# Half slots split their up weights on chip, and the rows of the next slot are turned inside the up products

## The chip, the cores and the metric

One NeuronCore of a Trainium2 chip runs the whole program. The metric is the device time of one execution in microseconds (us); a kernel's time is the median of its runs. The profiler records single executions, and every row below is of one such execution of the kernel before. The engines are PE (TensorE), DVE (VectorE), ACT (ScalarE), POOL (GpSimd) and SP (SyncE, which issues loads).

## The reference

4096 rows of 256 numbers go through four layers, each added to its own input: cross-attention, a mixture of experts with capacity, cross-attention, and a mixture in which each row goes to its two best of eight experts. Only the last one is touched:

```python
def _L1_ffn_ref(x, Wg, W11, W12, W2):          # Wg 256x8, W11/W12 8x256x512, W2 8x512x256
    gate_scores = softmax(x @ Wg)
    topk_scores, topk_idx = top_k(gate_scores, 2)
    topk_scores = topk_scores / (topk_scores.sum(-1, keepdims=True) + 1e-08)
    gate  = einsum('bsh,ehi->bsei', x, W11)
    value = einsum('bsh,ehi->bsei', x, W12)
    fused = gate * sigmoid(gate) * value
    expert_out = einsum('bsei,eih->bseh', fused, W2)
    gathered = take_along_axis(expert_out, topk_idx[..., None], axis=2)
    return sum(topk_scores[..., None] * gathered, axis=2)
x = x + _L1_ffn_ref(_layernorm(x), ...)
```

## The kernel before

The stage is `experts_top2` (lines 1342 to 1843); it begins at about 757 us of the trace and runs to the end. The 8192 pairs of a row and an expert have been sorted by expert in device memory. They are worked off in 32 **full slots** of 256 rows and 7 **half slots** of 128 rows, each slot of one expert. A loop of 7 passes (`body`) treats four full slots a, a+1, a+2, a+3 (a = 4j) and half slot j; `last` treats the remaining four. Products are in fp32 made of two parts: each factor is split into a "hi" copy and a "lo" rest, and three products (hi by hi, lo by hi, hi by lo) stand for one.

A full slot is, on PE: 4 transposes that turn its rows (L1481), `up` in four steps m = 0 to 3 of 12 matmuls (L1508), `down` of 24 matmuls (L1543). A half slot has 2 transposes (L1489), `half_up` of 12 matmuls 128x512 (L1521), a turn back (L1530) and `half_down` (L1555). PE's order in a pass is written out by hand:

```python
up(a);    transposes(a+1); down(a-1)
up(a+1);  transposes(a+2); down(a)
up(a+2);  half_transposes(j); down(a+1); half_up(j); transposes(a+3); down(a+2); half_turn(j)
up(a+3);  transposes(a+4); half_down(j)
```

Around it, for each full slot: ACT does the SiLU of each step m (L1632) and the hi copies of w2 (L1610), of the turned rows (L1614; half slot L1618) and of the hidden values (L1624). DVE multiplies gate and value (`hf`, L1752), does six small steps on weights and destinations (L1716 to L1721), and takes the lo rests: w2 (L1694), hidden values (L1689), rows (L1699; half slot L1704); it scales the outputs (L1738). POOL adds the scaled outputs to the result by indirect DMAs (`add`, L1812; half slot L1819). SP loads the sorted rows (L1435; half slot L1443), up weights of 2 MB per expert, already split into hi and lo in device memory (L1420, only when the expert changes), and w2 of 512 KB (L1428, likewise); before each it reads entries of a small table into registers (`entry`, L1404).

The up weights of a half slot, 2 MB, also come already split, in 8 pieces of 256 KB that ACT issues (L1599, queue q10): two at the fourth slot of the pass before, then two in each of a, a+1 and a+2. Its w2 comes in two pieces (L1605). Those of half slot 0 are issued ahead of the first slot. `half_up` waits for all 8 pieces.

The turned rows (xT_hi, xT_lo) have one buffer, so the rows of the next slot are turned only after `up` is over, and their split on ACT and DVE stands behind `up` too.

Of the kernel before, what the change touches and what calls it, by code (L numbers as in the profile page):

```python
# [15 lines left out]
P = 128  # L16
# [6 lines left out]
E = 8  # L23
# [14 lines left out]
NT1 = NF + NH + 1  # L38
# [429 lines left out]
def attention(p, layer, ins, setup, base, before):  # L468
# [423 lines left out]
    def plan(q):  # L892
# [51 lines left out]
        q.tensor_scalar(p.tab[:, 0, NF:NT1], row_o, float(IDLE_ROW), None, ALU.min).then_inc(s_tab, 1)  # L944
# [397 lines left out]
def experts_top2(p, ins, rows_from):  # L1342
# [11 lines left out]
    xT_hi, xT_lo = (at(k, x, [P, KC, T1], F32R) for k, x in ((56 + HALF, "xT_hi"), (58 + HALF, "xT_lo")))  # L1354
# [19 lines left out]
    hxin = at(60.5, "half_xin", [P, DW])  # L1374
    hxT_hi, hxT_lo = (at(k, x, [P, KC, P], F32R) for k, x in ((62 + HALF, "half_xT_hi"), (63 + HALF, "half_xT_lo")))
    hsg, hhf = (at(k, x, [P, F1]) for k, x in ((65, "half_sg"), (67, "half_hf")))
# [8 lines left out]
    sh_mt, sh_add = S("half_meta_steps"), S("half_rows_added")  # L1385
# [28 lines left out]
    def sync(q):  # L1414
        def load_up(i, par):
            e = entry(q, 1, i, E - 1)
            new = entry(q, 2, i, 1)
# [5 lines left out]
        def load_w2(i, par):  # L1423
            e = entry(q, 1, i, E - 1)
            new = entry(q, 2, i, 1)
# [4 lines left out]
        def load_x(i, par):  # L1430
            r = entry(q, 0, i, IDLE_ROW)
# [12 lines left out]

        def loads(i, par):
            load_x(i, par)
            load_up(i, par)
            load_w2(i, par)

        def body(j):  # L1450
            if not is_int(j):
                loads(4 * j + 1, 1)
            loads(4 * j + 2, 0)
            half_load_x(j)
            loads(4 * j + 3, 1)
            loads(4 * j + 4, 0)

        def last(a):
            for k in range(1, 4):
                loads(a + k, k % 2)  # L1460
        q.wait_ge(s_ahead, 16 * 4)
        q.wait_ge(rows_from.s_tab, 2)
        for i in range(2):
            load_up(i, i)
            load_w2(i, i)
        q.wait_ge(rows_from.s_tab, 3)
        rows_from.rows_landed(q)
        rows_from.tails_landed(q)
        for i in range(2):
            load_x(i, i)  # L1470
        slots(q, body, last)

    def tensor(q):
# [18 lines left out]
        def up(i, par, half=None, between=None):  # L1492
# [4 lines left out]
            for m in range(FC):  # L1497
                if m == 3 and between:
                    between()
                if m == 2 and half is not None:  # L1500
                    q.wait_ge(sh_hlo, half + 1)
                wait(q, s_hf, i * FC + m - 3)
                for v in range(2):
                    bank = ps[:, UP_BANK + m, v * T1:(v + 1) * T1]
                    k = 0
                    for c in range(KC):
                        for w, x in ((0, xT_hi), (0, xT_lo), (1, xT_hi)):
                            mm = q.matmul(bank, up_w[:, par, v, w, c, m * P:(m + 1) * P], x[:, c, :],  # L1508
                                          start=(k == 0), stop=(k == 3 * KC - 1))
                            k += 1  # L1510
                mm.then_inc(s_up, 1)

        def half_up(j):
            q.wait_ge(sh_xTlo, j + 1)
            q.wait_ge(sh_w, 16 * 8 * (j + 1))
            for v in range(2):
                q.wait_ge(s_hf, (4 * j + 2) * FC + v + 1)
                k = 0
                for c in range(KC):
                    for w, x in ((0, hxT_hi), (0, hxT_lo), (1, hxT_hi)):  # L1520
                        mm = q.matmul(ps[:, UP_BANK + v, :], x[:, c, :], hup[:, v, w, c, :],  # L1521
                                      start=(k == 0), stop=(k == 3 * KC - 1))
                        k += 1
                mm.then_inc(sh_up, 1)
# [34 lines left out]
        def body(j):  # L1559
            a = 4 * j  # L1560
            up(a, 0)
            transposes(a + 1, 1)
            if not is_int(j):
                down(a - 1, 1, j - 1)
            up(a + 1, 1)
            transposes(a + 2, 0)
            down(a, 0)
            up(a + 2, 0)
            half_transposes(j)
            down(a + 1, 1)  # L1570
            half_up(j)
            transposes(a + 3, 1, j)
            down(a + 2, 0)
            half_turn(j)
            up(a + 3, 1, j)
            transposes(a + 4, 0)
            half_down(j)

        def last(a):
            for k in range(3):  # L1580
                up(a + k, k % 2)
                transposes(a + k + 1, 1 - k % 2)
# [10 lines left out]
    def scalar(q):  # L1593
        def half_load_up(j, e, piece):

            v, w, c = piece // 4, piece // 2 % 2, piece % 2
            wait(q, sh_up, 2 * j)
            land(q, j)
            q.dma_start(hup[:, v, w, c, :].bitcast(F32), p.up1[e, :, v, w, c * F1:(c + 1) * F1]).then_inc(sh_w, 16)  # L1599

        def half_load_w2(j, e, piece):
            m = slice(piece * FC // 2, (piece + 1) * FC // 2)
            wait(q, sh_w2lo, j)
            land(q, j)
            q.dma_start(hw2[:, m, :], w2_d[:, e, m, :]).then_inc(sh_w2, 16)  # L1605
# [6 lines left out]
        def split_x(i, par):  # L1612
            q.wait_ge(s_xT, i + 1)
            q.activation(xT_hi[:, :, :], ps[:, X_BANK:X_BANK + KC, 0:T1], ACT.Copy).then_inc(s_xThi, 1)  # L1614
# [11 lines left out]
        def full(i, par, behind, ahead=None):  # L1626
            for m in range(FC):
                if ahead:
                    ahead(m)
# [11 lines left out]
        def half(j):  # L1641
# [10 lines left out]
        def body(j):  # L1652
            a = 4 * j
            e = None if is_int(j) else entry(q, 1, NF + j, E - 1)

            def ahead(first):
                def pieces(m):
                    if m % 2 == 1:
                        half_load_up(j, e, first + m // 2)
                    if m == 2 and first < 6:  # L1660
                        half_load_w2(j, e, first // 2 - 1)
                return None if is_int(j) else pieces

            def ahead_next(m):
                if m % 2 == 1:
                    half_load_up(j + 1, e_next, m // 2)
            full(a, 0, lambda: split_x(a + 1, 1), ahead(2))
            full(a + 1, 1, lambda: split_x(a + 2, 0), ahead(4))
            full(a + 2, 0, lambda: half_split_x(j), ahead(6))
            half(j)  # L1670
            e_next = entry(q, 1, NF + j + 1, E - 1)
            full(a + 3, 1, lambda: split_x(a + 4, 0), ahead_next)
# [5 lines left out]
        e = entry(q, 1, NF, E - 1)  # L1678
        for piece in range(8):
            half_load_up(0, e, piece)  # L1680
        for piece in range(2):
            half_load_w2(0, e, piece)
        slots(q, body, last)
        q.wait_ge(sh_w, 16 * (8 * NH + 2))

    def vector(q):
# [58 lines left out]
        def full(i, par, behind, output, between=False):  # L1745
            small = meta(i, par)
            for m in range(FC):
                if m == 3 and between:
                    output()
                q.wait_ge(s_sg, i * FC + m + 1)  # L1750
# [8 lines left out]
            behind()  # L1759
# [9 lines left out]
        def half(j):  # L1769
# [4 lines left out]
            split_x(4 * j + 3, 1)  # L1774
# [12 lines left out]
        def body(j):  # L1787
# [3 lines left out]
            full(a + 2, 0, lambda: half_split_x(j), lambda: outputs(a + 1, 1))  # L1791
# [11 lines left out]
    def gpsimd(q):  # L1803
# [17 lines left out]

        def body(j):
# [3 lines left out]
            add(a, 0)  # L1826
            add(a + 1, 1)
# [112 lines left out]
```

## Time and profile before

| | us |
|---|---|
| median of 3 runs | 1140.29 |
| the runs | 1137.93, 1140.29, 1145.8 |
| profiled execution, its own time | 1142.97 |
| its span | 1141.2 |
| the stage `experts_top2`, from the load of its first rows | 766.84 to the end |
| a pass with no weight load in its way (start of up(20) to start of up(24)) | 40.13 |

The mean granted clock of TensorE over the span is 0.964 of full speed. In the stage PE is busy for 92% of the time, DVE 64%, ACT 44%, POOL 30%.

### The profile page before, as it was taken

To read this page: it belongs to the slowest core of one execution; us is meant where nothing else is said; L and a number is where in the kernel's file an instruction comes from. 1 tells how busy PE (TensorE), PEld (TensorE's weight loads), DVE (VectorE), ACT (ScalarE), POOL (GpSimd) and SP (SyncE) were. 2 spreads that over 40 slices of the span, in tenths; PEclk is the share of its full clock that TensorE was granted. 3 is DMA by queue.
4 is the path that set the end of the run, shared out by engine and by line. 5 is a ranking of instruction groups with operands and counts; after the bars stand their busy time and mean duration, and the time that the engine had idled before them with its cause. 6 is when DMAs were issued, how large, how long until landed. Compare 5 with 4: busy or idle time off the path is not lost.

```text
span 1141.2 us, 24748 instructions
## 1 busy us (share of the span) xinstructions
PE 1033.3 (91%) x7562; PEld 955.1 (84%) x7562; DVE 720.7 (63%) x2241; ACT 661.5 (58%) x2450; POOL 509.4 (45%) x520
## 2 busy tenths in 40 slices
PE   6999998899999999889999999618999999899895
PEld 4688887799999998569999998617999989799795
DVE  6778886444444444866777777544756657576573
ACT  2788886444444443589999999304434444344351
POOL 1346776433333333345688886631232332333233
PEclk9999999899999999999999999757999999999898
DMA  9910002666666656101122221644868686757973
GB/s 315 341 52 25 29 30 72 259 223 226 220 228 221 226 187 202 34 20 38 48 72 74 71 69 55 255 149 122 243 143 285 161 268 179 209 141 232 320 222 71
DMA packets 101312, 180.69 MB, mean 158 GB/s; under 512 B 12898, under 2 KB 72932, under 8 KB 98788
## 3 DMA queue, kind: packets, MB, share of 16 engines
q1 hardware_dynamic: 71972, 133.13, 33.8%
q0 software_dynamic: 16368, 26.23, 10.5%
q10 hardware_dynamic: 12880, 20.21, 5.3%
q8 instruction: 44, 0.72, 0.3%
q14 instruction: 48, 0.39, 0.1%
HBM read 164.30 MB, written 62.43 MB: 199 GB/s over the span
## 4 chain that ended last, share of the span: by engine, by line
PE 75%; DMA 7%; DVE 7%; issue 4%; ACT 3%; SPq 2%; POOL 1%; ACTq 0%; DVEq 0%; POOLq 0%
PE psum L1508 12%; PE psum L696 11%; PE psum L679 11%; PE psum L1184 10%; PE psum L1201 10%; PE psum L1543 5%; DMA E_up_w<-up 4%; PE psum L651 4%; PE psum L1521 2%; DMA E_half_up_w<-up 2%; ACT L_prob L746 2%; PE psum L702 2%; PE psum L388 1%; DVE L_m_lo L440 1%; PE psum L666 1%
## 5 line engine op out<-in xcount | busy, mean ns | idle before, releaser
L746 ACT ACTIVATE L_prob<-psum,L_neg_max 128x64 f32<-128x64 f32 x768 | 229.3, 364 | 4.8 <-DVE L_neg_max L1003 4.7
L1812 POOL DMA_INDIRECT out<-E_y,E_dest x64 | 100.4, 1569 | 236.5 <-DVE E_y L1738 126.2
L1508 PE MATMUL psum<-E_xT_hi,E_up_w 128*128 128x256 f32 x1024 | 191.6, 286 | 14.3 <-DMA E_up_w<-up 7.3
L746 ACT ACTIVATION_READ_ACCUMULATOR L_prob<-psum,L_neg_max 128x1 f32 x768 | 196.3, 258 | 0.0
L1508 PEld LDWEIGHTS psum<-E_xT_hi,E_up_w 128*128 128x128 f32 x1024 | 162.3, 193 | 17.8 <-issue 11.6
L1508 PE MATMUL psum<-E_xT_lo,E_up_w 128*128 128x256 f32 x512 | 144.8, 283 | 0.0
L696 PE MATMUL psum<-L_n_hi,L_pT_hi 128*128 128x256 f32 x384 | 109.5, 285 | 9.8 <-DVE L_pT_lo L1010 9.8
L1632 ACT ACTIVATE E_sg<-psum 128x256 f32<-128x256 f32 x128 | 49.1, 384 | 117.7 <-PE psum L1508 109.8
L778 POOL TENSOR_TENSOR L_prob<-L_prob,L_rcp 128x512 f32<-128x512 f32 (+1 forms) x64 | 94.4, 1476 | 42.6 <-DVE L_rcp L969 41.2
L696 PE MATMUL psum<-L_n_hi,L_pT_lo 128*128 128x256 f32 x384 | 108.5, 282 | 0.0
L696 PE MATMUL psum<-L_n_lo,L_pT_hi 128*128 128x256 f32 x384 | 108.4, 282 | 0.0
L1242 ACT ACTIVATE E_h_hi<-psum 128x256 fp32r<-128x256 f32 (+1 forms) x128 | 55.7, 438 | 85.7 <-PE psum L1184 85.7
L1508 PEld LDWEIGHTS psum<-E_xT_lo,E_up_w 128*128 128x128 f32 x512 | 98.6, 193 | 0.0
L1752 DVE TENSOR_TENSOR E_hf<-psum,E_sg 128x256 f32<-128x256 f32 x128 | 53.9, 421 | 70.7 <-ACT E_sg L1632 68.9
L1285 DVE SCALAR_TENSOR_TENSOR E_h_lo<-psum,E_h_hi 128x256 fp32r<-128x256 f32 (+1 forms) x128 | 62.6, 491 | 53.8 <-ACT E_h_hi L1242 53.1
L1201 PE MATMUL psum<-E_w_hi,E_h_hi 128*128 128x256 f32 x320 | 90.0, 281 | 0.0
L1201 PE MATMUL psum<-E_w_hi,E_h_lo 128*128 128x256 f32 x320 | 89.4, 279 | 0.0
L1201 PE MATMUL psum<-E_w_lo,E_h_hi 128*128 128x256 f32 x320 | 89.4, 279 | 0.0
L696 PEld LDWEIGHTS psum<-L_n_hi,L_pT_hi 128*128 128x128 f32 x384 | 74.1, 193 | 13.5 <-issue 10.8
L679 PE MATMUL psum<-L_m_hi,L_xT_hi 128*128 128x512 f32 x192 | 81.9, 427 | 2.0 <-ACT L_prob L746 2.0
L1184 PE MATMUL psum<-E_xT_hi,E_w_hi 128*128 128x384 f32 (+1 forms) x256 | 78.8, 308 | 1.4 <-DVE E_xT_lo L1277 1.4
L1184 PE MATMUL psum<-E_xT_hi,E_w_lo 128*128 128x384 f32 (+1 forms) x256 | 78.8, 308 | 0.0
(248 smaller groups left out, 3141.1 us busy)
## 6 DMA issues: line engine op xcount, KB each, us to landing
E_up_w<-up SPq DMA_DIRECT2D x34, 2048.0 KB
E_w<-in_w SPq DMA_DIRECT2D x34, 512.0 KB
E_w<-in_w SPq DMA_DIRECT2D x16, 1024.0 KB, 7.2
E_half_up_w<-up ACTq DMA_DIRECT2D x58, 256.0 KB
E_xin<-rows SPq DMA_DIRECT2D x32, 260.0 KB
E_raw<-in_w SPq DMA_DIRECT2D x16, 512.0 KB, 6.6
up<-E_raw_hi SPq DMA_DIRECT2D x16, 512.0 KB, 6.3
up<-E_raw_lo SPq DMA_DIRECT2D x16, 512.0 KB, 4.0
```

The lines of the kernel that those rows point to most:

```text
L679: mm = e.matmul(bank, a[:, (t + 3) % 2, c, :], m[:, b, c, q * 512:(q + 1) * 512], start=(layer == 1 and c == 0 and j == 0), stop=(c == KC ...
L696: mm = e.matmul(o, a[:, r, :], m[:, b, r, :], start=(r == 0 and j == 0), stop=(r == PR - 1 and j == 2))
L746: last = e.activation(prob[q][:, h * KEYS:(h + 1) * KEYS], scores_ps(t)[:, h * KEYS:(h + 1) * KEYS], ACT.Exp, bias=nmx[:, q, h, :], accum_ ...
L778: e.tensor_tensor(pr, pr, rc[:, q, :, :].to_broadcast([P, H, KEYS]), ALU.mult).then_inc(s_p, 1)
L1184: mm = q.matmul(bank, a[par][:, c, m * P:(m + 1) * P], x[:, c, c0 * P:(c0 + cn) * P], start=(k == 0), stop=(k == 3 * KC - 1))
L1201: mm = q.matmul(bank, a[:, h, m, c * P:(c + 1) * P], w[par][:, m, :], start=(k == 0), stop=(k == 3 * FC - 1))
L1242: q.activation(h_hi[:, h, m, 0:cn * P], ps[:, UP_BANK + m % 4, 0:cn * P], ACT.Relu).then_inc(s_hhi, 1)
L1285: q.scalar_tensor_tensor(h_lo[:, h, m, 0:cn * P], ps[:, UP_BANK + m % 4, 0:cn * P], 0.0, h_hi[:, h, m, 0:cn * P].bitcast(F32), ALU.max, AL ...
L1508: mm = q.matmul(bank, up_w[:, par, v, w, c, m * P:(m + 1) * P], x[:, c, :], start=(k == 0), stop=(k == 3 * KC - 1))
L1543: mm = q.matmul(ps[:, Y_BANK + c, 0:D], a[:, par, m, c * P:(c + 1) * P], w[:, par, m, :], start=(k == 0), stop=(k == 3 * FC - 1))
L1752: q.tensor_tensor(hf[:, m, :], ps[:, UP_BANK + m, T1:2 * T1], sg[:, m, :], ALU.mult).then_inc(s_hf, 1)
L1812: q.indirect_dma_start(p.out[:, :], bass.IndirectOffsetOnAxis(ap=dest[:, par, c, :], axis=0), y[:, par, c, :], None, compute_op=ALU.add).t ...
```

## The change

It touches `experts_top2`, and the width of the table that `plan` writes (39 entries of slots in place of 40).

1. **Half slots' up weights.** Four raw pieces of 256 KB of w11 and w12 (1 MB) are loaded in place of eight split ones, issued by ACT after m = 1 and m = 3 of slots a and a+1. They are split on chip in slot a+2: ACT makes a hi copy of one piece after each step m (`half_split_up`), the first waiting for all four pieces; POOL takes the four lo rests, in its order behind the `add` of slot a and ahead of that of a+1. `half_up` waits for the four lo rests. w2 of the half slot is one load of 512 KB, issued at m = 1 of slot a+2. Nothing is loaded ahead of the first slot any more.
2. **Turned rows.** xT has two buffers. The transposes of slot i+1 stand at m = 2 inside up(i) (`turn`), their hi copy behind ACT's second SiLU, their lo rest ahead of DVE's third `hf`. In slot a+2 it is the half slot's transposes that stand there; those of a+3 come straight after up(a+2), ahead of down(a+1) and half_up, and they wait for the half slot's lo rest (`sh_xTlo`), since they write the same PSUM banks.
3. **SP.** The loads of up weights and w2 share one pair of table entries; entries are read ahead of the waits; those of the first two rows are read before the wait for the rows.

```diff
 def half_load_up(j, e, piece):
-    v, w, c = piece // 4, piece // 2 % 2, piece % 2
-    wait(q, sh_up, 2 * j)
+    v, c = piece // KC, piece % KC
+    wait(q, sh_wlo, 4 * j)
     land(q, j)
-    q.dma_start(hup[:, v, w, c, :].bitcast(F32), p.up1[e, :, v, w, c * F1:(c + 1) * F1]).then_inc(sh_w, 16)
+    q.dma_start(hraw[:, v, c, :], ins[("w11", "w12")[v]][e, c * P:(c + 1) * P, :]).then_inc(sh_w, 16)
+def half_split_up(j, piece):                      # ACT
+    v, c = piece // KC, piece % KC
+    q.wait_ge(sh_w, 16 * 4 * (j + 1))
+    wait(q, sh_up, 2 * j)
+    q.activation(hup[:, v, 0, c, :], hraw[:, v, c, :], ACT.Copy).then_inc(sh_whi, 1)
+def half_split_up(j, piece):                      # POOL
+    v, c = piece // KC, piece % KC
+    q.wait_ge(sh_whi, 4 * j + piece + 1)
+    q.tensor_tensor(hup[:, v, 1, c, :], hraw[:, v, c, :], hup[:, v, 0, c, :].bitcast(F32),
+                    ALU.subtract).then_inc(sh_wlo, 1)
 # PE
 def half_up(j):
     q.wait_ge(sh_xTlo, j + 1)
-    q.wait_ge(sh_w, 16 * 8 * (j + 1))
+    q.wait_ge(sh_wlo, 4 * (j + 1))
 def body(j):
-    up(a, 0)
-    transposes(a + 1, 1)
+    up(a, 0, turn=lambda: transposes(a + 1, 1))
     if not is_int(j):
         down(a - 1, 1, j - 1)
-    up(a + 1, 1)
-    transposes(a + 2, 0)
+    up(a + 1, 1, turn=lambda: transposes(a + 2, 0))
     down(a, 0)
-    up(a + 2, 0)
-    half_transposes(j)
+    up(a + 2, 0, turn=lambda: half_transposes(j))
+    transposes(a + 3, 1, j)
     down(a + 1, 1)
     half_up(j)
-    transposes(a + 3, 1, j)
     down(a + 2, 0)
     half_turn(j)
-    up(a + 3, 1, j)
-    transposes(a + 4, 0)
+    up(a + 3, 1, j, turn=lambda: transposes(a + 4, 0))
     half_down(j)
 # ACT, full(): in the loop over m
                 if m == 0:
                     split_w2(i, par)
+                if m == 1:
+                    behind()
                 if 0 < m < 3:
                     hidden_hi(i, par, m - 1)
-            behind()
+                if weights:
+                    weights(m)
 # DVE, full(): in the loop over m
+                if m == 2:
+                    behind()
                 q.wait_ge(s_sg, i * FC + m + 1)
 ...
-            behind()
 # POOL, body()
     add(a, 0)
+    for piece in range(4):
+        half_split_up(j, piece)
     add(a + 1, 1)
 # SP
-        load_x(i, par)
-        load_up(i, par)
-        load_w2(i, par)
+        r, e, new = entry(q, 0, i, IDLE_ROW), entry(q, 1, i, E - 1), entry(q, 2, i, 1)
+        load_x(i, par, r)
+        load_weights(i, par, e, new)
```

## Rows read from the trace of the kernel before

**Rows 1.** Page: the span, and the chain that ended last, by engine.
```profile
span 1141.2 us, 24748 instructions
PE 75%; DMA 7%; DVE 7%; issue 4%; ACT 3%; SPq 2%; POOL 1%; ACTq 0%; DVEq 0%; POOLq 0%
```

**Rows 2.** Windows: us; PE, PEld, DVE, ACT, POOL busy; clock; DMA share; GB/s.
```profile
768.00:1124.00 356.00, 327.70 (x2614) 318.24 (x2615) 229.45 (x686) 156.34 (x346) 105.09 (x67) 0.96 0.72 208
999.19:1039.32 40.13, 39.88 (x334) 39.10 (x335) 29.28 (x90) 19.77 (x44) 13.97 (x9) 1.00 0.56 124
```

**Rows 3.** Lines of PE, 768 to 1124 us: busy, mean ns, idle before and its releasers.
```profile
L1508 PE MATMUL psum<-E_xT_hi,E_up_w 128*128 128x256 f32 x1021 | 191.1, 286 | 14.3 <-DMA E_up_w<-up 7.3 <-DVE E_xT_lo L1699 6.8
...
L1521 PE MATMUL psum<-E_half_up_w,E_half_xT_hi 128*128 128x512 f32 x56 | 22.1, 458 | 12.5 <-DMA E_half_up_w<-up 12.5
```

**Rows 4.** Chain that ended last: start, us, step.
```profile
783.62 8.18 PE psum L1508 x48
...
871.67 10.44 DMA E_up_w<-up
...
975.90 7.18 DMA E_half_up_w<-up
983.21 4.60 PE psum L1521 x12
999.19 5.92 PE psum L1508 x48
...
1005.54 2.74 PE psum L1543 x24
1008.28 5.44 PE psum L1508 x48
...
1025.39 2.80 PE psum L1521 x12
...
1072.94 5.48 PE psum L1521 x12
```

**Rows 5.** Timeline of SP before the first slot (start, us, line; q: an issue).
```profile
760.94 0.12 SPq L1420 DMA_DIRECT2D E_up_w<-up  x1
762.51 0.09 SPq L1428 DMA_DIRECT2D E_w<-in_w  x1
...
766.84 0.41 SPq L1435 DMA_DIRECT2D E_xin<-rows  x1
```

**Rows 6.** Timeline of ACT and PE at slots 0 and 1; in brackets the idle before.
```profile
771.35 3.85 ACTq L1599 DMA_DIRECT2D E_half_up_w<-up  x8
...
776.61 1.28 ACT L1632 ACT_TABLE_LOAD   x1 [5.33 <-issue]
...
783.62 0.58 PE L1508 MATMUL psum<-E_xT_hi,E_up_w 128*128 128x256 f32 x1 [3.87 <-DVE E_xT_lo L1699]
```

**Rows 7.** Timeline of PE: first matmuls behind a wait, later in the stage.
```profile
907.10 0.38 PE L1508 MATMUL psum<-E_xT_hi,E_up_w 128*128 128x256 f32 x1 [0.24 <-DVE E_xT_lo L1699]
937.07 0.50 PE L1521 MATMUL psum<-E_half_up_w,E_half_xT_hi 128*128 128x512 f32 x1 [1.45 <-DMA E_half_up_w<-up]
983.21 0.79 PE L1521 MATMUL psum<-E_half_up_w,E_half_xT_hi 128*128 128x512 f32 x1 [4.92 <-DMA E_half_up_w<-up]
1072.94 0.79 PE L1521 MATMUL psum<-E_half_up_w,E_half_xT_hi 128*128 128x512 f32 x1 [4.64 <-DMA E_half_up_w<-up]
```

**Rows 8.** Timeline of ACT, DVE and POOL in slot 22 (its up runs from 1016.85).
```profile
1018.58 1.05 ACT L1610 ACTIVATE E_w_hi<-E_w 128x1024 fp32r<-128x1024 f32 x1
1020.61 0.16 DVE L1719 SCALAR_TENSOR_TENSOR E_mb<-E_xin,shift 128x2 f32<-128x2 f32 x1
1020.68 1.22 DVE L1694 TENSOR_TENSOR E_w_lo<-E_w,E_w_hi 128x1024 fp32r<-128x1024 f32 x1
1021.82 0.42 DVE L1689 TENSOR_TENSOR E_h_lo<-E_hf,E_h_hi 128x256 fp32r<-128x256 f32 x1
1023.42 0.41 DVE L1704 TENSOR_TENSOR E_half_xT_lo<-psum,E_half_xT_hi 128x256 fp32r<-128x256 f32 x1
1019.24 1.55 POOL L1812 DMA_INDIRECT out<-E_y,E_dest  x1 [0.30 <-issue]
```

**Rows 9.** Timeline of ACT in slot 14 (its up runs from 926.66).
```profile
931.01 1.06 ACT L1610 ACTIVATE E_w_hi<-E_w 128x1024 fp32r<-128x1024 f32 x1 [2.25 <-DMA E_w<-in_w]
```

**Rows 10.** One source line of POOL: count, then ns min/median/max and span.
```profile
L1322 POOL TENSOR_TENSOR E_raw_lo<-E_raw,E_raw_hi x16: 2396/2404/2419, 223.9 to 435.5; 128x1024 fp32r<-128x1024 f32 x16
```

**Rows 11.** Timeline of DVE and POOL, and the source line of this DVE instruction.
```profile
494.51 1.27 DVE L1018 SCALAR_TENSOR_TENSOR x<-L_got,factor,x 128x256 f32<-128x256 f32 x1
493.60 1.91 POOL L778 TENSOR_TENSOR L_prob<-L_prob,L_rcp 128x1024 f32<-128x1024 f32 x1 [8.68 <-DVE L_rcp L969]
L1018 DVE SCALAR_TENSOR_TENSOR x<-L_got,factor,x x32: 451/454/1273, 459.2 to 683.7; 128x256 f32<-128x256 f32 x32
```

More of the change, by code:

```diff
@@ L1353, in experts_top2 @@
     w2_hi, w2_lo = (at(k, x, [P, 2, FC, D], F32R) for k, x in ((40, "w2_hi"), (48, "w2_lo")))
[L1354 removed]
+    xT_hi, xT_lo = (at(k, x, [P, 2, KC, T1], F32R) for k, x in ((56 + HALF, "xT_hi"), (60 + HALF, "xT_lo")))
     xin = at(82, "xin", [P, 2, TC, DW])
@@ L1384, in experts_top2 @@
         S("half_" + x) for x in ("up", "silu", "h", "hT", "hT_hi", "hT_lo", "down", "y_scaled"))
-    sh_mt, sh_add = S("half_meta_steps"), S("half_rows_added")
+    sh_mt, sh_add, sh_whi, sh_wlo = (S("half_" + x) for x in ("meta_steps", "rows_added", "w1_hi", "w1_lo"))
     def nth(i):
@@ L1414, in sync, with load_weights @@
     def sync(q):
-        def load_up(i, par):
-            e = entry(q, 1, i, E - 1)
-            new = entry(q, 2, i, 1)
+        def load_weights(i, par, e, new):
             wait(q, s_up, FC * (i - 1))
@@ L1428, in load_w2, with load_x @@
             q.dma_start(w2[:, par, :, :], w2_d[:, e, :, :], cond=new).then_inc(s_w2[par], 16)
-        def load_x(i, par):
-            r = entry(q, 0, i, IDLE_ROW)
+        def load_x(i, par, r):
             wait(q, s_mt, NM * (i - 1))
@@ L1463, in sync @@
         for i in range(2):
-            load_up(i, i)
-            load_w2(i, i)
+            load_weights(i, i, entry(q, 1, i, E - 1), entry(q, 2, i, 1))
         q.wait_ge(rows_from.s_tab, 3)
+        r = [entry(q, 0, i, IDLE_ROW) for i in range(2)]
         rows_from.rows_landed(q)
@@ L1490, in half_transposes, with up @@
             mm.then_inc(sh_xT, 1)
-        def up(i, par, half=None, between=None):
+        def up(i, par, half=None, turn=None, between=None):
             q.wait_ge(s_xTlo, i + 1)
@@ L1497, in up @@
             for m in range(FC):
+                if m == 2 and turn:
+                    turn()
                 if m == 3 and between:
@@ L1580, in last @@
             for k in range(3):
-                up(a + k, k % 2)
-                transposes(a + k + 1, 1 - k % 2)
+                up(a + k, k % 2, turn=lambda: transposes(a + k + 1, 1 - k % 2))
                 down(a + k - 1, 1 - k % 2, NH - 1 if k == 0 else None)
@@ L1613, in split_x @@
             q.wait_ge(s_xT, i + 1)
-            q.activation(xT_hi[:, :, :], ps[:, X_BANK:X_BANK + KC, 0:T1], ACT.Copy).then_inc(s_xThi, 1)
+            q.activation(xT_hi[:, par, :, :], ps[:, X_BANK:X_BANK + KC, 0:T1], ACT.Copy).then_inc(s_xThi, 1)
         def half_split_x(j):
@@ L1624, in hidden_hi, with full @@
             q.activation(h_hi[:, par, m, :], hf[:, m, :], ACT.Copy).then_inc(s_hhi, 1)
-        def full(i, par, behind, ahead=None):
+        def full(i, par, behind, weights=None):
             for m in range(FC):
-                if ahead:
-                    ahead(m)
                 q.wait_ge(s_up, i * FC + m + 1)
@@ L1653, in body, with load, split @@
             a = 4 * j
[L1654 to L1669, printed above, removed]
+            e = entry(q, 1, NF + j, E - 1)
+            def load(first):
+                return lambda m: half_load_up(j, e, first + m // 2) if m % 2 else None
+            def split(m):
+                half_split_up(j, m)
+                if m == 1:
+                    half_load_w2(j, e)
+            full(a, 0, lambda: split_x(a + 1, 1), load(0))
+            full(a + 1, 1, lambda: split_x(a + 2, 0), load(2))
+            full(a + 2, 0, lambda: half_split_x(j), split)
+            split_x(a + 3, 1)
             half(j)
-            e_next = entry(q, 1, NF + j + 1, E - 1)
-            full(a + 3, 1, lambda: split_x(a + 4, 0), ahead_next)
+            full(a + 3, 1, lambda: split_x(a + 4, 0))
         def last(a):
@@ L1677, in scalar @@
         split_x(0, 0)
[L1678 to L1682, printed above, removed]
         slots(q, body, last)
-        q.wait_ge(sh_w, 16 * (8 * NH + 2))
     def vector(q):
```

35 lines of the change are left out of this document (15 added, 20 removed).

## The prediction

> **What bounds the kernel now.** I read the chain that ended last first: three quarters of the span is PE [rows 1], so a gain must come out of PE's idle time or out of work taken off PE. The change takes none off: the matmuls and transposes are as many as before. So I looked next at the windows: in the stage PE is busy for 327.7 of 356.0 us, at a clock of 0.96, and in a pass that no weight load disturbs for 39.9 of 40.1 us [rows 2]. The reader is to see that everything the change can give lies in those 28 us and in the clock. The lines of PE say where they are: 12.5 us ahead of half_up, all of it for pieces of the half slot's weights; 7.3 us ahead of up for its own weights; 6.8 us ahead of up for the lo rest of the turned rows [rows 3]. The chain shows what a wait costs beyond itself: half_up takes 2.80 us after none, 4.60 after the wait of 4.92, 5.48 after that of 4.64; up takes 5.44 in the flow and 5.92 behind a short wait [rows 4, 7].
>
> **What the change takes away.**
>
> - SP's start. SP issues five loads between 760.94 and 766.84, each up weight or w2 load 1.5 us after the one before, the last after 1.3 [rows 5]; two table entries stand in each step of 1.5, one in the last. Two pairs go, one entry moves ahead: at about 0.55 each that is 4 less 1, 1.6 us (bounds 0, if another wait stands there too, and 2.2).
> - The start of ACT. Ten issues hold ACT from 771.35 to 776.6, then a table load of 1.28; slot 0's chain of SiLU, hf and split comes that much later, PE waits 3.87 us for up(1), which then takes 8.18 instead of 5.92 [rows 4, 6]. Both go: 3.9 + 2.3 = 6.2.
> - The waits for turned rows at the end of a pass: 0.24 [rows 7], six like it of 0.24 to 0.29, 1.5 in all; the up behind each drops from 5.92 to 5.44 [rows 4], 6 x 0.48 = 2.9.
> - half_up's waits for pieces: 12.5 [rows 3], and the two slow half_ups, 1.8 + 2.7 = 4.5 [rows 4]. The lo rests that it waits for now are made in slot a+2; their cover is checked below. 17.0.
> - Up's waits for its own weights, 7.3 [rows 3]: half slots load 1 MB instead of 2 per pass, but these waits stand where 2 MB loads take 10.44 us to land [rows 4], and that stays so. I take 4 (bounds 0 and 7.3).
>
> Together 33.2 us.
>
> **What it adds.** In a pass PE now goes from up(a+2) straight to the transposes of a+3, and these wait for the half slot's lo rest. PE works in order, so down(a+1) and half_up stand behind this wait, and nothing covers it. Before, down(a+1), 2.74 us, lay between. What that rest waits for is a chain over ACT, DVE and POOL:
>
> Slot 22 shows it without loads in the way. Counted from the start of its up (1016.85): w2's hi copy ends at 2.8; DVE takes w2's lo rest from 3.8 to 5.05, a lo rest of hidden values to 5.4, then hf; the half rows' rest at present is done at 7.0; POOL's add ends at 3.9 [rows 8]. Up ends at 5.44. In the new order the half rows are turned at m = 2 and their rest stands behind w2's lo and the first h lo. ACT's first copy of 128x512 goes in between, about 0.6 (half of the 1.05 of 128x1024 [rows 8], with some fixed part), so hf and w2's lo come 0.6 later, at 4.4; the rest would be ready at 4.4 + 1.22 + 0.42 + 0.41 less overlaps, about 6.0: PE idles 0.6 us.
>
> But POOL now works in the same stretch. A subtract of 128x1024 takes it 2.40 us [rows 10], so each of the four of 128x512 about 1.2, and they start right behind the add, at 4.0. The trace has one place where DVE begins an instruction with two inputs in SBUF while such a POOL instruction runs: POOL runs from 493.60 to 495.51, DVE's instruction, else 0.45, takes 1.27 and ends 0.27 after POOL's [rows 11]. It was kept waiting for the whole of POOL's. w2's lo rest and the h lo rests have two inputs in SBUF. So I count, as the likeliest order: first subtract 4.0 to 5.2; DVE's last small step, which has SBUF inputs too, is held until then; the second subtract takes over until 6.45; w2's lo to 7.7; the third subtract to 8.9; the first h lo to 9.2; the half rows' rest to 9.5. PE is idle for about 3.9 us.
>
> The Trainium skill ("SBUF — State Buffer", section "Who interferes with whom") gives the reason: the second SBUF input of a DVE instruction and GpSimd's reads use one shared port pair, whichever began first keeps it to its end, and ScalarE is never held up. By that rule a quiet slot idles 1.8 to 3.9 us according to who begins first; by durations alone it is 0.6; the trace agrees with the rule in the 1.27 us above.
>
> The sum of what is lost:
>
> - Quiet slots a+2 (2, 6, 22): 3 x 3.9 = 11.7 (bounds 3 x 0.6 and that).
> - Slots a+2 with a new expert (10, 14, 18, 26). There w2 lands late: ACT's hi copy starts 4.35 us after up begins, in slot 14, having waited 2.25 [rows 9], against 1.7 in slot 22 [rows 8]. Part of the first subtract is then over before DVE comes, but all later steps start 2 us or so later: rest ready at about 8.5 without a lock, 9.7 with it, and somewhat earlier where the smaller traffic lets w2 land sooner. I take 3.0 each, 12 (bounds 1.5 and 4.5).
> - Clock after such a stall: the two waits of 4.6 to 4.9 cost 2.2 us on average behind them, those under 1.5 nothing [rows 4, 7]. For seven stalls of 3 to 4 us I take 1.3 each, 9 (bounds 0 and 15).
> - Transposes at m = 2 in slots with a new expert (5, 9, 13, 25): the rows of the next slot are queued on SP behind the w2 that is late [rows 9], and at m = 2, some 2.7 us after up began, they may not be there. 4 x 0.6 = 2.5 (bounds 0 and 6).
>
> Together 35.2. POOL's lo rests are done at about 10.2 to 11; half_up starts behind the stall, the transposes and down(a+1), at 9.5 + 0.4 + 2.74 = 12.7: covered by 2 us. The net is +2.0: 1142.97 + 2 = 1145 in the profiled execution's terms. The median of the runs lies 2.7 lower, so 1142.
>
> **The rivals.**
>
> - *DVE goes first.* If w2's lo rest gets in ahead of a subtract, or the small steps are not held, a quiet slot idles about 2.1 instead of 3.9, which costs little clock: 3 x 1.8 + 4 x 0.6 + some 5 of clock, 13 less: 1129 to 1130. For it: the POOL start (4.0) and DVE's (4.4) are 0.4 apart, with a semaphore on either side. Against it: ACT's new copies make DVE later, not earlier.
> - *No lock here.* The instructions of [rows 11] are of other forms. Then quiet slots idle 0.6 (10 less), the others 1.8 (5 less), and the clock stays (7 less): 1120.
> - *ScalarE waits for the raw pieces* (the slower side). ACT's first split, behind m = 0 of a+2, waits for all four pieces, and every SiLU stands behind it. The last piece is issued at about the end of up(a+1), 2.8 us before up(a+2) begins. It delays nothing while it lands before w2's hi copy ends, at 5.4 in slots with a new expert: within 8.2 us. Beyond, each us of landing costs PE one in those four passes. Pieces landed 7.18 us after issue in the worst pass [rows 4]. At the 10.44 of a 2 MB load it would be 4 x 2.2 us and as much clock again as one stall in two brings, 12 in all: 1154. Against it: 1 MB less to move.
> - The skill's page "DMA: Bandwidth & Descriptors", section "Queues, rings and completion order", speaks against this rival: engines alternate between rings packet by packet, so ACT's 256 KB would not stand behind SP's 2 MB. The 7.18 beside the 10.44 agrees.
>
> **How the numbers follow.** The forecast with the stall as worked out: 0.48, with a range of its own from 1132 to 1150. DVE first: 0.28. No lock: 0.12. Late pieces: 0.12. The time is that of the first, 1142. A measurement of this kernel tells about 1% from no change: 1128.9 and 1151.7. Faster by more: nearly all of "no lock" and half of "DVE first", 0.27. Slower by more: late pieces and the upper tail of the first, 0.17. The rest 0.56. The range from 1121 to 1154 leaves out about half of "no lock", a third of "late pieces" and the tails.
>
> **What the profile would show.** Right: ahead of the transposes L1481 that follow up(a+2) PE idles 2.5 to 4.5 us for the half slot's lo rest on DVE, in every pass, with a clock under 1 behind it; DVE's w2 lo takes over 2 us there, and POOL's subtracts alternate with it; no wait ahead of half_up; up(1) without its wait of 3.9. Wrong: if w2's lo stays at 1.2 us beside a running subtract, there is no lock; if the idle time stands behind ACT's split with q10 as its releaser, the pieces are late; if half_up waits for POOL, the subtracts take longer than 1.2 us or start later.

## The result, and the profile after

| | before | after |
|---|---|---|
| median, us | 1140.12 (4 runs) | 1175.71 (4 runs) |
| profiled execution, its own time | 1142.97 | 1176.07 |
| its span | 1141.2 | 1174.3 |
| ratio of the times, 95% interval | | 1.030, 1.027 to 1.034 |
| first load of rows to the end of the span | 374.4 | 406.4 |

The kernel became slower by 36 us, beyond the upper end of the range, 1154. The stage holds 32 of the 33 us by which the two profiled executions differ.

The page's span, the chain that ended last by engine, and the first entries by line:

```profile
span 1174.3 us, 24457 instructions
PE 69%; DVE 10%; DMA 8%; issue 6%; ACT 4%; POOL 1%; SPq 1%; ACTq 0%; DVEq 0%; POOLq 0%
PE psum L679 11%; PE psum L696 10%; PE psum L1184 10%; PE psum L1201 10%; PE psum L1505 7%; PE psum L1540 6%; PE psum L651 3%; DVE E_wt L1705 3%; DMA E_xin<-rows 3%; DMA E_w<-in_w 2%; PE psum L388 2%; DMA out<-E_y,E_dest 2%; ACT L_prob L746 2%; PE psum L702 2%; PE psum L1518 2%
```

Against [rows 1], PE's share of the chain fell from 75 to 69%, DVE's rose from 7 to 10%. What is new in it is `E_wt L1705`: DVE's third small step, on 128x2 numbers, has 3% of the chain.

Lines of PE and DVE and the POOL subtracts, from the start of the stage (columns as in [rows 3]):

```profile
L1505 PE MATMUL psum<-E_xT_hi,E_up_w 128*128 128x256 f32 x1024 | 194.9, 284 | 7.4 <-DMA E_up_w<-up 5.9 <-DVE E_xT_lo L1686 1.4
L1475 PE MATMUL psum<-ident,E_xin 128*128 128x128 f32 x128 | 23.4, 314 | 50.1 <-DVE E_half_xT_lo L1691 41.8 <-DMA E_xin<-rows 8.4
L1518 PE MATMUL psum<-E_half_up_w,E_half_xT_hi 128*128 128x512 f32 x56 | 18.7, 395 | 0.0
L1483 PE MATMUL psum<-ident,E_half_xin 128*128 128x128 f32 x14 | 2.9, 288 | 2.1 <-DMA E_half_xin<-rows 2.1
L1705 DVE TENSOR_TENSOR E_wt<-E_ma,E_xin 128x2 f32<-128x2 f32 x32 | 41.4, 1295 | 0.0
L1812 POOL TENSOR_TENSOR E_half_up_w<-E_half_raw,E_half_up_w 128x512 fp32r<-128x512 f32 x28 | 38.5, 1792 | 0.0
```

half_up (L1518) waits for nothing; in [rows 3] it waited 12.5 us. Up's waits for turned rows are down to the first slot's 1.4. But the transposes (L1475) wait 41.8 us for the half slot's lo rest, seven stalls of 5.15 to 6.61, one per pass. And the small step is booked with 41.4 us for 32 instructions: 25 of them take the usual 0.15, so the seven in slots a+2 take 5.4 each. It had no idle time before it: it had begun and did not end. POOL's line has a second point: 28 records of 1.79 us make 50.2, but POOL was busy with them for 38.5, so the records of its subtracts overlap.

One pass of it, slot 22 as in [rows 8] (its up runs from 1041.07). First the timeline of POOL, then of DVE, then of PE:

```profile
1043.67 1.54 POOL L1799 DMA_INDIRECT out<-E_y,E_dest  x1 [0.31 <-issue]
1044.68 5.53 POOL L1812 TENSOR_TENSOR E_half_up_w<-E_half_raw,E_half_up_w 128x512 fp32r<-128x512 f32 x4
...
1044.84 0.43 DVE L1741 TENSOR_TENSOR E_hf<-psum,E_sg 128x256 f32<-128x256 f32 x1 [0.90 <-ACT E_sg L1627]
1045.18 5.05 DVE L1705 TENSOR_TENSOR E_wt<-E_ma,E_xin 128x2 f32<-128x2 f32 x1
1050.27 0.16 DVE L1706 SCALAR_TENSOR_TENSOR E_mb<-E_xin,shift 128x2 f32<-128x2 f32 x1
1050.35 1.22 DVE L1681 TENSOR_TENSOR E_w_lo<-E_w,E_w_hi 128x1024 fp32r<-128x1024 f32 x1
1051.48 0.42 DVE L1676 TENSOR_TENSOR E_h_lo<-E_hf,E_h_hi 128x256 fp32r<-128x256 f32 x1
1051.82 0.42 DVE L1691 TENSOR_TENSOR E_half_xT_lo<-psum,E_half_xT_hi 128x256 fp32r<-128x256 f32 x1
...
1052.38 0.45 PE L1475 MATMUL psum<-ident,E_xin 128*128 128x128 f32 x1 [5.27 <-DVE E_half_xT_lo L1691]
```

The reader is to see two ends side by side: POOL's row of four ends at 1050.21, DVE's small step at 1050.23. Three changes from one subtract to the next lay in between, and DVE got in at none. By the records there was no gap to get into: each subtract begins 1.2 to 1.4 us after the one before it, and 0.5 to 0.6 us before that one ends (0.4 in slot 2). The spans that a profile gives for POOL are rough, so this does not show that no gap existed. Behind the small step w2's lo, the h lo and the half rows' rest take their usual times, and PE starts.

In slot 18, one with a new expert, the row of four stands later. POOL and DVE:

```profile
994.00 1.55 POOL L1799 DMA_INDIRECT out<-E_y,E_dest  x1 [8.13 <-DMA out<-E_y,E_dest]
...
996.87 5.49 POOL L1812 TENSOR_TENSOR E_half_up_w<-E_half_raw,E_half_up_w 128x512 fp32r<-128x512 f32 x4
...
996.52 5.87 DVE L1705 TENSOR_TENSOR E_wt<-E_ma,E_xin 128x2 f32<-128x2 f32 x1
```

POOL's add ahead of the row had waited for earlier adds to land, so the row begins 6.0 us after the start of up (990.83; 3.6 us in slot 22) and DVE meets all of it. The small step's record even begins 0.35 us ahead of the row's (0.13 in slot 10, 0.20 in slot 26), and it is held to the end all the same.

What comes behind such a stall, in the chain and in windows (columns as in [rows 2]); the last two hold the lowest and the highest clock behind a stall:

```profile
1052.38 1.08 PE psum L1475 x4
1053.47 4.49 PE psum L1540 x24
...
1053.00:1060.00 7.00, 7.00 (x37) 6.60 (x36) 2.99 (x8) 1.53 (x5) 2.20 (x2) 0.71 0.24 46
1020.00:1040.00 20.00, 20.00 (x174) 20.00 (x174) 15.99 (x47) 11.02 (x27) 5.23 (x4) 1.00 0.53 103
802.19:809.19 7.00, 7.00 (x33) 6.82 (x34) 3.58 (x11) 1.32 (x3) 1.71 (x2) 0.59 0.80 281
852.59:859.59 7.00, 7.00 (x39) 6.55 (x40) 3.58 (x11) 2.06 (x5) 1.92 (x2) 0.78 0.20 42
```

The clock granted from 1053 to 1060 is 0.71, in the undisturbed stretch 1.00; over the 7 us from the end of each of the seven stalls it is 0.59 to 0.78. The transposes take 1.08, and down(a+1) 4.49 instead of the 2.74 of [rows 4].

### The profile page after: what moved, and what is told of

Its sections match the earlier page's. It is cut to its first block, busy times and chain, and to the rows that moved or that the text cites. A ratio compares the mean times of both kernels' runs of the same rounds, so it can differ in the third digit from the quotient of the medians.

```text
span 1174.3 us, 24457 instructions
## 1 busy us (share of the span) xinstructions
PE 1042.0 (89%) x7562; PEld 963.8 (82%) x7562; DVE 762.1 (65%) x2241; ACT 678.4 (58%) x2478; POOL 543.2 (46%) x548
## 3 DMA queue, kind: packets, MB, share of 16 engines
q1 hardware_dynamic: 71972, 133.13, 32.7%
q0 software_dynamic: 16368, 26.23, 10.3%
## 4 chain that ended last, share of the span: by engine, by line
PE 69%; DVE 10%; DMA 8%; issue 6%; ACT 4%; POOL 1%; SPq 1%; ACTq 0%; DVEq 0%; POOLq 0%
PE psum L679 11%; PE psum L696 10%; PE psum L1184 10%; PE psum L1201 10%; PE psum L1505 7%; PE psum L1540 6%; PE psum L651 3%; DVE E_wt L1705 3%; DMA E_xin<-rows 3%; DMA E_w<-in_w 2%; PE psum L388 2%; DMA out<-E_y,E_dest 2%; ACT L_prob L746 2%; PE psum L702 2%; PE psum L1518 2%
## 5 line engine op out<-in xcount | busy, mean ns | idle before, releaser
L1505 PE MATMUL psum<-E_xT_hi,E_up_w 128*128 128x256 f32 x1024 | 194.9, 284 | 7.4 <-DMA E_up_w<-up 5.9
L778 POOL TENSOR_TENSOR L_prob<-L_prob,L_rcp 128x512 f32<-128x512 f32 (+1 forms) x64 | 94.5, 1476 | 43.2 <-DVE L_rcp L969 41.8
L1621 ACT ACTIVATE E_h_hi<-E_hf 128x256 fp32r<-128x256 f32 x128 | 53.1, 415 | 50.3 <-DVE E_hf L1741 49.2
```

The source lines that it names most:

```text
L778: e.tensor_tensor(pr, pr, rc[:, q, :, :].to_broadcast([P, H, KEYS]), ALU.mult).then_inc(s_p, 1)
```

## The experiments

The theory, called "held" in the expectations: POOL's four subtracts run without a break; a DVE instruction with two SBUF inputs that meets them is held to the end of the last one; and the half rows' rest stands behind that instruction in DVE's order. The rival, "too early": the transposes of a+3 stand too early for a chain over ACT that the change itself made late, and the profile only books the waiting on the small step.

| kernel | against before, 95% interval | wait of the transposes for the half rows' rest, us | wait of half_up, us |
|---|---|---|---|
| the changed kernel | 1.030, 1.027 to 1.034 | 41.8 | 0 |
| rest_first | 1.005, 1.003 to 1.008 | 2.7 | 10.3 |
| subtract_gap | 1.001, 0.998 to 1.003 | 18.0 | 3.5 |
| dve_split | 0.991, 0.988 to 0.994 | 5.3 | 8.0 |
| turn_only | 0.993, 0.990 to 0.996 | 2.2 | 3.6 |
| split_only | 1.021, 1.018 to 1.025 | (behind half_up) | 38.8 |
| eight | 1.027, 1.023 to 1.032 | 41.2 | 0 |
| dve_order | 0.998, 0.996 to 1.000 | 10.6 | 1.8 |
| dve_split_late | 0.991, 0.989 to 0.993 | 5.4 | 7.8 |
| dve_order_late | 0.998, 0.995 to 1.000 | 9.5 | 1.5 |

The kernel before ran beside each of them; its medians were 1144.39, 1142.77 and 1145.56 in the three groups (rest_first to turn_only; eight, split_only, dve_order; the two late ones), so the ratios are to be compared, not the medians.

**rest_first: the half rows' rest ahead of the small step.**

```diff
 # DVE, full() of slot a+2
     hf(1)
+    half_split_x(j)
     small.more(2); split_w2; hidden_lo(0)
-    half_split_x(j)
     hf(2)
```

> The changed kernel, but in slot a+2 DVE takes the half rows' lo rest right behind the second hf, ahead of its third small step, of w2's lo rest and of the first h lo; everything else in place, POOL's four subtracts too. Theory 'held' (POOL's four subtracts run without a break, and DVE's small step that begins while they run is held to the end of the last, 5 us, with the half rows' rest behind it in DVE's order): the small step still takes about 5 us, but the rest is ready before it, so the 41.8 us ahead of the transposes that follow up(a+2) fall to under 10 and the clock behind them recovers; half_up then waits up to 1 us for POOL, down(a+2) about 1 us for h lo: 1125 to 1140 us. Rival 'too early' (the transposes of a+3 stand too early in PE's order for the chain over ACT, whose copies and late w2 make everything late, and the long small step is only where the profile books it): the rest waits for ACT's hi copy as before, the stall stays above 4 us per pass, over 1165 us.

Median 1152.57. The 41.8 fell to 2.7 us, so the chain over ACT was in time: "too early" falls. The subtracts and the hold stayed. Timeline of POOL and DVE in slot 22:

```profile
1030.59 5.58 POOL L1814 TENSOR_TENSOR E_half_up_w<-E_half_raw,E_half_up_w 128x512 fp32r<-128x512 f32 x4
...
1031.10 0.41 DVE L1691 TENSOR_TENSOR E_half_xT_lo<-psum,E_half_xT_hi 128x256 fp32r<-128x256 f32 x1
1031.43 4.77 DVE L1705 TENSOR_TENSOR E_wt<-E_ma,E_xin 128x2 f32<-128x2 f32 x1
```

Both DVE instructions meet running subtracts. The one that reads PSUM and one SBUF tile takes its 0.41 us; the one that reads two SBUF tiles takes 4.77 instead of 0.15. The gain was smaller than expected, because the held DVE is late for others: half_up waited 10.3 us for POOL and down(a+2) 9.5 us for the outputs behind DVE's late lo rests, where I had allowed some 14 for both, and the clock drops behind some of these too (0.59 over 848.79 to 855.79, 0.77 over 946.77 to 953.77). That is some 6 us more than allowed; the rest of the 13 us above the expected range is not accounted for.

**subtract_gap: one break in POOL's row.**

```diff
 # POOL, body()
-    for piece in range(4):
+    half_split_up(j, 0)
+    q.wait_ge(s_w2lo, a + 3)
+    for piece in range(1, 4):
         half_split_up(j, piece)
```

> The changed kernel, but POOL, after its first subtract, waits for w2's lo rest of slot a+2 before the other three: one break in its row of four. 'Held': the small step is held for at most the first subtract (1.3 us or less), w2's lo follows at once, and the half rows' rest comes at about 7.4 us after up begins, so that PE waits about 2 us per pass in place of 6; half_up may wait up to 1 us for POOL; 1135 to 1150 us. If each POOL subtract let DVE in between anyway, the break would change nothing: 1175. 'Too early': 1170 to 1176.

Median 1145.04, within the expectation. Slot 22, POOL and DVE:

```profile
1022.91 1.87 POOL L1812 TENSOR_TENSOR E_half_up_w<-E_half_raw,E_half_up_w 128x512 fp32r<-128x512 f32 x1
...
1023.41 1.40 DVE L1705 TENSOR_TENSOR E_wt<-E_ma,E_xin 128x2 f32<-128x2 f32 x1
...
1024.92 1.22 DVE L1681 TENSOR_TENSOR E_w_lo<-E_w,E_w_hi 128x1024 fp32r<-128x1024 f32 x1
...
1026.30 4.06 POOL L1812 TENSOR_TENSOR E_half_up_w<-E_half_raw,E_half_up_w 128x512 fp32r<-128x512 f32 x3 [1.52 <-ACT E_half_up_w L1602]
...
1026.39 0.42 DVE L1691 TENSOR_TENSOR E_half_xT_lo<-psum,E_half_xT_hi 128x256 fp32r<-128x256 f32 x1
...
1026.96 0.63 PE L1475 MATMUL psum<-ident,E_xin 128*128 128x128 f32 x4 [1.62 <-DVE E_half_xT_lo L1691]
...
1027.06 0.56 DVE L1707 TENSOR_TENSOR E_mb<-E_mb,spare 128x2 f32<-128x2 f32 x1
1027.65 1.22 DVE L1708 TENSOR_TENSOR E_mb<-E_mb,E_xin 128x2 f32<-128x2 f32 x1
```

With the break, the small step is held for one subtract, and PE waits 1.62 instead of 5.27. In the row of three behind the break DVE and POOL then take turns: the next two small steps are held for one subtract each (ends at 1027.62 and 1028.87), and these three records do not overlap by more than 0.04 us.

The break fell into the row in four passes of seven (slots 2, 18, 22 and 26), and all four look like this. In slots 6, 10 and 14 w2's lo was done before POOL began, so the row of four ran unbroken and held a small step (L1707) for 5.5 us, but the half rows' rest was done by then. In slots 10 and 14 the transposes still waited 4.4 and 4.3: there DVE had stood 6.1 and 6.0 us, until 884.00 and 932.23, for adds that had not landed, ahead of the slot's first hf. This is another limit; it comes back below.

**dve_split: no subtract on POOL.**

```diff
 # POOL, body()
-    for piece in range(4):
-        half_split_up(j, piece)
 # DVE, behind the h lo rests of slot a+2
+    for piece in range(4):
+        half_split_up(j, piece)      # the same subtract, on DVE
```

> The changed kernel, but DVE itself takes the four lo rests of the half slot's up weights (4 of 128x512, about 0.7 us each), behind the h lo rests of slot a+2; POOL only adds. 'Held': small step back at 0.15 us, the stall ahead of the transposes falls to 0.6 in slots without a new expert and 1 to 2 in the others, and half_up waits 1 to 2 us per pass for DVE's subtracts: 1130 to 1145 us. 'Too early': the stall stays above 4 us per pass and the four subtracts come on top: over 1170.

Median 1133.89: faster than both kernels, by 0.9% (0.6 to 1.2) against before. Lines of PE and DVE:

```profile
L1475 PE MATMUL psum<-ident,E_xin 128*128 128x128 f32 x128 | 20.4, 283 | 16.3 <-DMA E_xin<-rows 11.0 <-DVE E_half_xT_lo L1691 5.3
L1518 PE MATMUL psum<-E_half_up_w,E_half_xT_hi 128*128 128x512 f32 x56 | 19.4, 407 | 8.0 <-DVE E_half_up_w L1735 6.9 <-issue 1.1
L1735 DVE TENSOR_TENSOR E_half_up_w<-E_half_raw,E_half_up_w 128x512 fp32r<-128x512 f32 x28 | 17.4, 684 | 0.0
L1705 DVE TENSOR_TENSOR E_wt<-E_ma,E_xin 128x2 f32<-128x2 f32 x32 | 4.9, 152 | 0.1
```

The small step is back at 0.152 us, and the stall at 0.4 in slots without a new expert (the prediction's 0.6 for "no lock") and about 1.0 in the others. The four subtracts take 2.5 us of DVE per pass; PE's waits ahead of the transposes and half_up sum to 13.3 us, against 41.8 with the subtracts on POOL.

**turn_only: parts 2 and 3 alone.**

```diff
 # against the changed kernel
-    raw pieces, half_split_up on ACT and POOL
+    8 split pieces from up1 per half slot, 2 of w2, those of half slot 0 ahead of slot 0
```

> Parts 2 and 3 of the change alone: rows turned inside up into two buffers, transposes of a+3 straight behind up(a+2), SP's entries; the half slots' weights come split in 8 pieces with the loads ahead of the first slot, as in the kernel before. 'Held': no POOL subtract, so no small step above 0.3 us and a stall ahead of the transposes of 0.6 in quiet slots, 1 to 2 in those with a new expert; half_up's waits of 12.5 us and the wait of 3.9 at the start are back: 1132 to 1145 us. 'Too early': the stall stays at 4 to 6 us per pass: over 1165.

Median 1136.63, faster than before, with the transposes at exactly the place where they cost 41.8 us in the changed kernel. They wait 2.2 us here: the place alone is not the cause. half_up's waits came back with only 3.6 us, not 12.5, and up(1)'s with 2.0, not 3.9; I had not expected that, and no run looked into it.

**split_only: parts 1 and 3 alone.**

```diff
 # against the changed kernel: the rows are turned where they were before
-    up(a+2, turn=half_transposes); transposes(a+3); down(a+1); half_up
+    up(a+2); half_transposes; down(a+1); half_up; transposes(a+3)
```

> Parts 1 and 3 of the change alone: raw pieces split by ACT and POOL, no loads ahead of the first slot, SP's entries; the rows are turned behind up as in the kernel before, and the transposes of a+3 stand behind half_up again. 'Held': DVE's third small step still takes about 5 us in slot a+2, and w2's lo, two h lo, two hf and the half rows' rest come behind it, at about 12 to 13 us after up began; PE meets it at half_up, which has down(a+1) ahead of it, at 8.5: a wait of 3.5 to 5 us per pass there, 25 to 35 us in all, and clock behind it: 1150 to 1175 us, so part 1 without part 2 already makes the kernel slower than before. If it is the new place of the transposes that costs the time, this kernel has no stall over 1 us in quiet slots and runs in 1120 to 1135 us.

Median 1165.97. Line of PE:

```profile
L1518 PE MATMUL psum<-E_half_up_w,E_half_xT_hi 128*128 128x512 f32 x56 | 29.2, 595 | 38.8 <-DVE E_half_xT_lo L1695 38.8
```

The stall has only moved behind down(a+1): 38.8 us ahead of half_up. In each pass a small step of DVE (L1709, once L1710) was held for 5.1 to 6.2 us. So part 1, the split on POOL, makes the kernel slower whether or not the rows are turned early. The parts do not add: +2.1% and -0.7% against +3.0% for both. Each alone already takes most of the 12.5 us of half_up's waits for pieces, which can be gained only once; the rest of the difference is not accounted for.

**eight: more boundaries.**

```diff
 # POOL
-    one subtract of 128x512 per piece
+    two subtracts of 128x256 per piece
```

> The changed kernel, but POOL takes its lo rests in eight subtracts of 128x256 instead of four of 128x512: the same work with seven boundaries in place of three, and ACT's hi copies as before. If DVE is kept out because POOL's next subtract always stands ready at a boundary, more boundaries change nothing: the third small step still takes 5 to 6 us per pass, the stalls ahead of the transposes sum to 40 to 50 us, 1172 to 1185 us. If DVE gets in at a boundary by chance or by turn, eight short subtracts must let it in early: small step under 2 us, stalls under 20 us, below 1150 us.

Median 1172.88 (two runs); the stalls sum to 41.2. Slot 10 first, then slot 22, DVE:

```profile
895.23 0.20 DVE L1705 TENSOR_TENSOR E_wt<-E_ma,E_xin 128x2 f32<-128x2 f32 x1
895.46 5.91 DVE L1706 SCALAR_TENSOR_TENSOR E_mb<-E_xin,shift 128x2 f32<-128x2 f32 x1
...
1044.80 0.67 DVE L1706 SCALAR_TENSOR_TENSOR E_mb<-E_xin,shift 128x2 f32<-128x2 f32 x1
1045.39 1.85 DVE L1681 TENSOR_TENSOR E_w_lo<-E_w,E_w_hi 128x1024 fp32r<-128x1024 f32 x1
```

In six passes of seven one small step is held across all that is left of the eight. In slot 22 DVE and POOL took turns: each DVE instruction was held for about one short subtract (0.67 where 0.16 is usual, 1.85 where 1.22 is), and that pass stalled 2.1 us only. So taking turns, on which the prediction was built, does occur: once in these 7 passes, in the four of subtract_gap with a break, and in none of the 7 of the changed kernel.

Over the five kernels with subtracts on POOL a DVE instruction was held to the end of the row in 30 of 35 passes, and in each of the 30 the records of the subtracts overlap by 0.4 to 0.6 us. Where DVE got in, they overlap by 0.04 at most (four passes of subtract_gap, in which the row of three began with POOL idle and not right behind an add), but in slot 22 of this kernel by 0.6 and more. So the hold goes with overlapping subtracts, with one exception; what decides it was not tried and stays open. In the first two passes ACT's hi copies ended within 0.1 us of the same times as in slot 22, counted from POOL's start, and there DVE was held to the end.

**dve_order, dve_split_late, dve_order_late: what bounds next.** dve_order orders DVE's work in slot a+2 by what PE needs first; the late ones move the copy of the destinations.

```diff
 # dve_order, DVE in slot a+2
-    hf(1); small; w2 lo; h lo(0); half rest; hf(2); ...; h lo(3); 4 subtracts
+    hf(1); half rest; small; hf(2); small; hf(3); 4 subtracts; w2 lo; h lo(0..3)
 # *_late, DVE
-    wait(q, s_add, 16 * TC * (i - 1)); copy of dest(i)    # at the end of slot i
+    the same behind hf(1) of slot i + 1 (for a+2: in the half slot)
```

> DVE takes the four lo rests of the up weights (as in dve_split), and in slot a+2 its order is by what PE needs first: the half rows' rest behind the second hf, then the other hf, the four subtracts, and only then w2's lo and the four h lo rests. In dve_split 5.3 us ahead of the transposes and 8.0 us ahead of half_up remained. If these came from DVE's order, the transposes wait under 2 us in all and half_up under 4, with at most 0.5 us per pass given back ahead of down(a+2), and the median falls by 5 to 10 us below dve_split, to 1120 to 1130. If DVE as a whole is full there, the waits only move to down(a+2): 1131 to 1137.

> dve_split (DVE takes the four lo rests), and DVE's copy of a slot's destinations, which waits until the adds of two slots before have landed, is moved from the end of the slot to behind the second hf of the next one (for slot a+2, into the half slot), about 2 to 3 us later in DVE's order. In dve_split DVE idled 7.4 us there. If the landing of the adds is the next limit only by that place in DVE's order, these waits fall under 3 us and the median by 1 to 4 us, to 1130 to 1133; if DVE's wait was hidden behind PE's, nothing moves: 1133 to 1135.

> dve_order with the same move of the copy of destinations. In dve_order DVE idled 32.5 us ahead of these copies, for adds that had not landed, and the transposes behind up(a+2) waited up to 7 us in slots 10 and 26. If the late adds are what took the gain of that order, the 32.5 falls below 15, the transposes wait under 4 us in all, and the median comes to 1122 to 1131, below dve_split. If the adds themselves bound the passes, the wait only moves to the new place: 1134 to 1140.

Medians 1139.77, 1135.57 and 1141.95. All three lie above what was expected, the first by 2.8 us, the second by 0.6, the third by 2.0. The copies of destinations, DVE, in dve_order and in dve_order_late:

```profile
L1766 DVE CAST E_dest<-E_mb 128x2 int32<-128x2 f32 x32 | 5.2, 163 | 32.5 <-DMA out<-E_y,E_dest 32.5
...
L1770 DVE CAST E_dest<-E_mb 128x2 int32<-128x2 f32 x32 | 6.3, 197 | 13.8 <-DMA out<-E_y,E_dest 13.8
```

half_up's wait fell as meant, from 8.0 to 1.8, but DVE stood 32.5 us for adds that had not landed, and with it the half rows' rest (in slot 26 PE waited 7.0 us). Moving the copy took DVE's wait from 32.5 to 13.8 in dve_order_late and from 7.4 to nothing in dve_split_late, and the time did not follow in either. In slot 26 of dve_order_late DVE still stood 7.68 us at the new place and PE 6.55 behind it: there the adds themselves are late, and the wait only moved. Why they land late there was not tried. The best version found is dve_split; dve_split_late does not differ from it.

## Why the prediction was wrong

**The place and the mechanism held.** PE stood where the prediction put it, at the transposes behind up(a+2), for the half rows' rest, in all seven passes and with nothing covering it; DVE was kept out by POOL's subtracts through its second SBUF input; half_up did not wait for POOL; up(1)'s 3.87 was gone. "No lock" is refuted by L1705. "DVE goes first" did not save a pass: in slots 10, 18 and 26 the small step's record begins first, and it was held all the same. The raw pieces were not late; the copies of all 28 pieces stand in the lines of ACT without any idle time before them:

```profile
L1602 ACT ACTIVATE E_half_up_w<-E_half_raw 128x512 fp32r<-128x512 f32 x28 | 17.6, 630 | 0.0
```

**The step that failed** is the order at the boundaries: "first subtract 4.0 to 5.2; DVE's last small step ... is held until then; the second subtract takes over until 6.45; w2's lo to 7.7". I let DVE in after each subtract. It was held to the end of the fourth, 4.9 to 5.9 us instead of 1.2 at most, and PE stood 41.8 us instead of 23.7. [rows 11] show one POOL instruction and one DVE instruction; that a held instruction is let in at the next boundary was my own addition, and no row of before showed two POOL instructions in a row against a waiting DVE.

The term for slots with a new expert failed on a second point. It took 3.0 us for each, less than the 3.9 of a quiet slot, because "part of the first subtract is then over before DVE comes". POOL's row was late there too: it began 5.3 to 6.0 us after up and not at 4.0, behind an add that had waited for earlier adds, and DVE met all or nearly all of it. These four stalls are the longer ones, 6.3 to 6.6 us against 5.2 to 5.4. The terms of the sum:

| term | predicted, us | measured, us |
|---|---|---|
| stalls ahead of the transposes | 11.7 + 12 = 23.7 | 41.8 |
| clock behind them | 9 | about 15 |
| rows not there at m = 2 | 2.5 | 2.0 + 2.1 for the half slots' rows |
| half_up's waits, and their clock | -17.0 | waits -12.5, no slow half_up left |
| up's waits for its weights | -4 | -1.4 (7.3 to 5.9) |
| SP's start | -1.6 | -1.8 |
| ACT's start | -6.2 | -4.5 (start of up(0) to end of up(1), 19.7 to 15.2) |
| waits for turned rows, and the ups behind | -4.4 | waits -1.5; the ups were not measured |

The 15 is from the chain: transposes 1.08 instead of 0.44 in each of seven, and downs of 3.7 to 5.0, on average 4.2, instead of 2.74, so 7 x (0.64 + 1.47). The 1.8 is the time from the end of SP's last stores ahead of the stage (L619) to the first load of rows, 8.3 against 6.5; the prediction's 0.55 per table entry does not follow from [rows 5], where a step with two entries takes 1.5 and the one with a single entry 1.3, so that it came out was luck. That end itself came 2.9 later in the profiled execution of after, in code that the change leaves alone. The losses add up to 61, against 35.2; what is left as gain, 61 less the 30 by which the profiled executions differ from there on, is 31, against 33.2. So the gain was sized about rightly and the loss was not.

**The range was too narrow on the same step.** The prediction bounded the stall of a quiet slot by 0.6 and 3.9 us, with 3.9 itself as the upper end. A bound from above was at hand in its own rows: hold DVE for all four subtracts, 4.0 + 4 x 1.2 = 8.8, and w2's lo, one h lo and the rest behind it, at about 10.7, a stall of 5.2 in quiet slots and as much or more elsewhere. With the 2.2 us of clock of [rows 4] behind each, that is 7 x 7.4 = 52 instead of 32.7 us, and 1161 us for the median, still 15 short of the measured one. The Trainium skill ("SBUF — State Buffer", section "Who interferes with whom") says that whoever issues first keeps the port pair for the whole instruction. The trace agrees for one instruction (1.40 us held in subtract_gap), but not on who is first by the starts of the records (slots 10, 18 and 26); of several in a row the section says nothing, and here the hold ran through four.

**Smaller points.** The 1.2 us for a subtract of 128x512 was nearly right as a spacing: the four begin 1.2 to 1.4 us apart. One record lasts 1.6 to 1.9, so the row of four takes 5.4 to 5.6 us and not 4.8. The prediction also gives a quiet slot's idle time with DVE ahead of POOL once as 1.8 and once as 2.1; 1.8 is the difference from 3.9, and only the 2.1 fits its sum for that rival.

## What to carry to other kernels

Work given to GpSimd is not free for VectorE: where a stretch has several GpSimd instructions that read SBUF back to back, count a VectorE instruction with two SBUF inputs that meets them, however small, as held to the end of the last one (so it was in 30 of 35 passes here), and look at what stands behind it in VectorE's order. Put first what other engines wait for and what reads PSUM (rest_first took 39 us off one wait by moving one instruction), or give the work to VectorE itself (dve_split). A break in GpSimd's row helps only where it falls into the row: in subtract_gap in four passes of seven. And where a rival engine has a queue of ready work, take the whole queue as the upper bound, not one instruction of it.

## What the runs showed of the hardware that I had not expected

- A DVE instruction on 128x2 numbers took 4.6 to 6.2 us, against 0.15, through four POOL subtracts in a row (after, rest_first, split_only); with eight shorter ones it was held for 5.4 to 6.1 in six passes of seven, and in one pass the two engines took turns.
- Subtracts that begin right behind an add overlap by 0.4 to 0.6 us in their records; a row that began with POOL idle (subtract_gap) did not, and there DVE got in after each.
- A DVE instruction with one input in PSUM and one in SBUF ran at its usual 0.41 us amid the same subtracts.
- A stall of PE of 5.15 to 6.6 us was followed by a granted clock of 0.59 to 0.78 over the next 7 us, and cost about 2 us there.
